# Sums of the softmaxes brought to query rows by eight transposes of the evicted values

## What is computed

```python
scores = jnp.einsum('bhqd,bhkd->bhqk', q, k) / SCALE
attn = jax.nn.softmax(scores, axis=-1)
out_std = jnp.einsum('bhqk,bhkd->bhqd', attn, v)
scores_p = jnp.einsum('bhqd,bhkd->bhqk', q, kp) / SCALE
attn_p = jax.nn.softmax(scores_p, axis=-1)
out_p = jnp.einsum('bhqk,bhkd->bhqd', attn_p, v)
out = alpha * out_std + (1.0 - alpha) * out_p
out = out.transpose(0, 2, 1, 3).reshape(B, T, C)
return out @ W_O.T
```

## Time and profile before

| | us |
|---|---|
| median of 3 runs | 4743.82 |
| lowest and highest run | 4728.14, 4755.17 |
| the profiled execution | 4749.89 |
| its span, first to last instruction | 4748.1 |
| attention block of the change, within the span | about 2435 to 3003 |
| first and last SUMS | 2515.3, 2992.4 |

### The profile page before, as it was taken

How to read it: one execution, slowest core, us unless ns; L and a number is a source line. 1 busy time by engine, 2 the same in 40 slices (tenths; PEclk the granted TensorE clock), 3 DMA queues, 4 the chain that set the end, 5 groups by cost and what they waited for, 6 DMA issues and landing times. The chain is left out here.

```text
span 4748.1 us, 152747 instructions
## 1 busy us (share of the span) xinstructions
PE 4417.7 (93%) x67272; PEld 2900.6 (61%) x67272; DVE 3454.7 (73%) x4473; ACT 2463.9 (52%) x2820; POOL 2399.2 (51%) x3067
## 2 busy tenths in 40 slices
PE   8999978999999999999969999799999999999997
PEld 6666656666666666666633333466666666666665
DVE  3333348888888888888757776588888888888885
ACT  1121115666566666556516665355666656656664
POOL 0000016666666666666523232366666766666663
PEclk8988989999999999999968787799999999999998
DMA  1000012222322222232200000222222232222221
GB/s 60 9 9 18 9 50 62 74 65 68 78 67 75 73 72 64 67 81 62 65 0 1 1 1 1 60 62 67 75 70 72 67 82 67 70 72 69 72 67 50
DMA packets 150987, 255.73 MB, mean 54 GB/s; under 512 B 37321, under 2 KB 41041, under 8 KB 150225
## 3 DMA queue, kind: packets, MB, share of 16 engines
q1 hardware_dynamic: 150352, 246.30, 19.6%
HBM read 50.09 MB, written 1.05 MB: 11 GB/s over the span
## 5 line engine op out<-in xcount | busy, mean ns | idle before, releaser
L608 PE MATMUL psum<-loc_wqkv,loc_zs 128*128 128x512 f32 x2304 | 1124.8, 612 | 21.1 <-DVE loc_zs L1157 15.6
L608 PEld LDWEIGHTS psum<-loc_wqkv,loc_zs 128*128 128x128 f32 x2304 | 405.6, 193 | 374.8 <-issue 332.0
L963 POOL TENSOR_TENSOR loc_rc_k<-loc_rc_k,loc_rs_k 128x1024 f32<-128x1024 f32 x192 | 454.6, 2368 | 151.8 <-DVE loc_rs_k L1044 151.6
L703 PEld LDWEIGHTS psum<-loc_PT,loc_V 64*64 64x64 f32 x24576 | 393.5, 135 | 203.5 <-issue 201.8
L703 PE MATMUL psum<-loc_PT,loc_V 64*64 64x32 f32 x24576 | 423.8, 220 | 56.5 <-issue 49.4
L963 POOL TENSOR_TENSOR loc_rc_q<-loc_rc_q,loc_rs_q 128x1024 f32<-128x1024 f32 x192 | 453.7, 2363 | 0.0
L841 ACT ACTIVATE loc_sq_k<-psum 128x1024 f32<-128x1024 f32 x192 | 196.7, 1025 | 478.9 <-PE psum L608 478.9
L722 PEld LDWEIGHTS psum<-loc_outT,loc_wo 128*128 128x128 f32 x3072 | 380.0, 195 | 98.8 <-issue 91.5
L938 POOL TENSOR_TENSOR loc_rt<-loc_rn 128x32 f32<-128x32 f32 x192 | 46.2, 240 | 689.7 <-DVE loc_rn L1040 680.7
L722 PE MATMUL psum<-loc_outT,loc_wo 128*128 128x128 f32 x3072 | 380.0, 278 | 1.9 <-DVE loc_gg L1100 1.9
L969 POOL TENSOR_TENSOR loc_qk_q<-loc_rc_q,loc_rn 128x1024 f32<-128x1024 f32 x192 | 365.5, 1904 | 26.7 <-issue 0.4
(11 more groups left out here) (178 smaller groups left out, 9165.8 us busy)
## 6 DMA issues: line engine op xcount, KB each, us to landing
loc_V<-loc_V SPq DMA_DIRECT2D x1152, 128.0 KB, 2.4
loc_V<-loc_V SPq DMA_DIRECT2D x672, 64.0 KB, 2.1
loc_wqkv<-in_wqkv SPq DMA_DIRECT2D x42, 512.0 KB, 3.8
moe_w<-in_moe_w SPq DMA_DIRECT2D x32, 256.0 KB, 3.4
loc_wo<-in_wo SPq DMA_DIRECT2D x12, 512.0 KB, 4.4
loc_w<-in_w SPq DMA_DIRECT2D x12, 341.0 KB, 3.2
loc_w<-in_w SPq DMA_DIRECT2D x12, 192.0 KB, 3.2
loc_scales<-in_scales SPq DMA_DIRECT2D x14, 128.0 KB, 3.4
```

Of the source, the lines that this page charges most:

```text
L608: mm = pe.matmul(M.bank[bank + g], zs[:, s, i * P:(i + 1) * P], wqkv[:, k, g * T:(g + 1) * T], start=True, stop=True)
L703: mm = pe.matmul(M.bank[WB + c][64 * j:64 * j + 64, m * P + q:m * P + q + 32], V2[r:r + 64, i, w, p * 64:(p + 1) * 64], PT[r:r + 64, p, q: ...
L963: pool.tensor_tensor(rc[:, :], rc[:, :], rs[:, :], ALU.add).then_inc(added, 1)
```

## The change

The eight products with four moving columns become eight transposes of the same blocks of `raw` by the identity. They fill all 512 columns of both banks of the pair instead of 32 columns of one, and the reciprocal reads every 32nd column (column 8 of each head's 32) from the two banks. The four selecting columns leave the constant `sel`. Nothing moves: on every engine the same number of program lines stands in the same order, with the same waits.

```diff
-    HI, SELECTED, SIGNS, SUM_ROW = 3 * AD, 4, 6, 8
+    HI, SELECTED, SIGNS, SUM_ROW = 3 * AD, 0, 2, 4
...
-                    bank = take_pair(a_nth["sums", u])[0]
+                    pair = take_pair(a_nth["sums", u])
                     pe.wait_ge(values_out, 2 * u + 2)
                     for y in range(2):
                         for i in range(TILES):
-                            col = (y * TILES + i) * 4
-                            mm = pe.matmul(bank[:, col:col + 4], raw[:, y, i * P:(i + 1) * P], M.sel[:, 0:4],
-                                           start=True, stop=True)
+                            mm = pe.transpose(pair[y][:, i * P:(i + 1) * P], raw[:, y, i * P:(i + 1) * P], M.ident[:, :])
                     mm.then_inc(a_full, 1)
...
                     dve.wait_ge(a_full, n + 1)
-                    dve.reciprocal(recip[:, :, :, :].rearrange("p y i r -> p (y i r)"), B[A_PAIRS[n % 2][0]][:, 0:8 * TILES]).then_inc(a_free, 1)
+                    b = A_PAIRS[n % 2][0]
+                    dve.reciprocal(recip[:, :, :, :].rearrange("p y i r -> p y (i r)"),
+                                   M.psum[:, b:b + 2, :].rearrange("p y (r e) -> p y r e", e=32)[:, :, :, AD]).then_inc(a_free, 1)
...
-    sums = np.arange(P)[:, None] == np.arange(4)[None, :] * 32 + AD
...
-    return np.concatenate([sums] + chosen + signs + [row == AD], 1).astype(np.float32)
+    return np.concatenate(chosen + signs + [row == AD], 1).astype(np.float32)
```

More of the change, by code:

```diff
@@ L1498, in program @@
         M.wv_full = sb("wv_full", [P, D])
-        M.sel = sb("sel", [P, 9])
+        M.sel = sb("sel", [P, 5])
         M.wo_full = sb("wo_full", [P, 4 * D])
```

## The result

| | before | after |
|---|---|---|
| median of 4 runs, us | 4745.09 | 4662.99 |
| lowest and highest | 4728.14, 4755.17 | 4659.95, 4675.46 |
| span of the profiled execution | 4748.1 | 4661.8 |
| mean granted clock over it | 0.942 | 0.961 |

A forecast was written before the change was run, and what follows sets the result against it. Clock falls after SUMS were taken to bound the attention block: 65 us from 13 units, 5 from the next, 2.5 from the last two, 72 in sum, less 6 for remaining falls, 66: 4743.8 to 4678, range 4652 to 4720.

The forecast's parts named there:

- What bounds the kernel: Attention block: 14 half-clock stretches, 174.1 us, each beginning 1.06 to 4.16 us after a SUMS start, blamed on few streaming columns.
- This is on the path: VectorE waits for SUMS; eight transposes replacing its products shorten it from 1.88 to 1.02 us, 0.86 per unit, 13.8 in all.
- The reciprocal at 0: Reading 32 values per row at a stride from two banks costs nothing extra; at most 2.8 us allowed.
- The clock, argued from BACK: Six low stretches end during BACK's eight transposes, so transposes in SUMS should make the fall vanish in most units.
- Rival 1: The clock falls all the same after SUMS; only the shortening of 13.8 us is left, 4729; chance 0.12.
- The unit at full clock, 27.0 us: Attention unit without low clock: 27.9 us, less 0.86 for the shorter SUMS; 13 units take 351 instead of 416.3 us.
- The price of low clock: An attention unit was reckoned 0.30 to 0.31 us longer per us at half clock.
- I don't believe in none: Two or three of 14 units still fall, at SUMS or behind BACK, 7 us at half each; 6 us taken back.
- Rival 2: Half of the falls stay, halving the clock's share: 43 us gained, 4701; chance 0.09.
- Rival 3: Slower: the fall moves behind BACK and the clock stays at half through OUT, TURN and projections; up to 4768; chance 0.03.
- The lower end, 4652,: Low stretches at VectorE's full-clock share, 108 us instead of 174, plus 14 and 3: 83 us, and half the run spread below.
- It can't get much better than that: After the change VectorE is late, with 23.1 us of work in a unit of 27.0, the rest its waits.

The follow-up runs named there:

- full_products: The changed kernel with its eight SUMS transposes made ordinary products by the same identity, 16 instructions of 128 columns; ratio 0.9844, 13 units 360.0 us.
- half_sums: The kernel before with only the first softmax's sums made, 8 instructions of four columns, reciprocals used for both; ratio 0.9963, 13 units 399.5 us.
- filler_mixed: The kernel before with eight unread transposes added, each directly behind one of the eight four-column products in SUMS; ratio 0.9942, 13 units 398.0 us.

## Why the prediction was right

The forecast was 4678 with a range of 4652 to 4720; it is 4663. The medians fell by 82 us where 66 were forecast. Of the 16 us between, 6 are the falls that I expected to stay, 4 or 5 lie in the size of other terms of the block, and the rest lies outside the block, in code that the change doesn't touch, and is no merit or fault of the forecast.

- **What bounds the kernel:** right. The falls were the cost, and the four columns at a time brought them, where SUMS stands: full_products and half_sums, which change the one without the other, show it. They are not the whole cause, since one step later only 10 of 14 falls come. Two details of the prediction were inexact. The engine had not always "just done 16 instruction pairs": ten of the 14 falls come 1.06 to 1.9 us after the start of SUMS, while the pairs are still running. And the idle 0.69 us is not right ahead of SUMS; L1306 stands between for 1.0 us.
- **"This is on the path", 0.86 us per unit:** right. The units of full_products and after differ by 0.96 us, of which 0.10 is that 16 instructions with 128 columns take 1.98 us and not 1.88.
- **The reciprocal at 0:** right, 357 ns and 358 ns in the median.
- **The clock, argued from BACK:** right. The transposes of SUMS and BACK together hold the clock at 1.00 in 13 units. The sentence of the Trainium skill named against it ("TensorE: Matmul & The Clock Gate", Part 4, PE-mode transpose) doesn't fit the float32 transposes of this kernel: full_products and after keep the clock alike, though one has ordinary products and the other transposes in SUMS, while half_sums, whose SUMS of 1.0 us has next to no columns, falls 14 times. Rival 1 is out.
- **The unit at full clock, 27.0 us:** a little high. It measured 26.73 on average (347.5 / 13), 3.5 us over 13 units. The 27.9 us before the shortening were the high part: units without a fall take 27.6 us with 32 or 64 columns. The price of low clock, put at 0.31 us per us, was low: it comes out at 0.36 from half_sums (52 us more than after in 13 units, which hold 143.5 of its 157.2 us low) and at 0.35 from before against full_products (56.3 for 160.4).
- **"I don't believe in none":** this was the mis-sized term. I had taken back 6 us for two or three units that still fall, because the idle times around SUMS and BACK stay. None fell, in this traced execution or in that of the kernel's second run. Sum without it: 72 us, and the block measured 76.5: 68.8 in the 13 units against 65, 5.6 in the next against 5, and 2.1 in the last two against 2.5.
- **Rival 2** (half of the falls stay) did not happen here, but it is what 32 columns give. **Rival 3** (the falls move behind BACK) has nothing for it: in every trace the falls between the first SUMS and the end of the maxima come 0.8 to 4.3 us after the start of a SUMS, ahead of its BACK.
- **The lower end, 4652,** doesn't follow from its own terms: 4743.8 - 83 = 4661, less half of the spread of the runs (13.5) is 4647. The result lies inside by either.
- **"It can't get much better than that":** too strong. Moving SUMS and BACK by a step each took 0.4 and 0.3 us more off the unit in the traces.

What stays open: why the kernel with four columns has only 10 falls instead of 14 when SUMS stands one step later, why filler_mixed keeps its late falls, and what exactly of columns, rows, idle time and the place of SUMS against the points at which the clock changes adds up to a fall. The counts between 0 and 14 are of one execution each. The runs show the order of the cases, not a rule.

## What to carry to other kernels

Where TensorE is busy by the page and its granted clock is below 1.00, cut the block at the points where the clock changes and look what ran just ahead of each. Groups of products with few moving columns are weight loads with little behind them. If the loads set their length anyway, give them as many columns as the output has room for, or use single transposes: 16 instructions with 128 columns took 1.98 us here, with four 1.88 us, and the wide ones gave back 56 us in 13 units. Dummy work behind such a group did not help here: 12 of 14 falls stayed, and the kernel became slower.

## What the runs showed of the hardware

- Sixteen float32 loads of 128x128 with their products take 1.88 us with 4 moving columns, 1.91 with 32, 1.93 with 64 and 1.98 with 128 (at the full clock, to the start of the next product). What differs is the clock afterwards: 14, 8, 2 and 0 falls.
- The same 24 instructions bring 12 falls when the eight with many columns stand behind the sixteen with four, and 8 when they are mixed.
- At the low clock, an attention unit costs about 0.35 us more per microsecond, not a whole one: VectorE is still busy 52% of the time there, against 84% at the full clock.
